# A Mamba block with a mixture of experts: the delta product in bf16, the routing's top two in PSUM, other instruction orders and banks, and 40 idle transposes at the start

## The reference

```python
xi, res = jnp.split(layernorm(x) @ W_in, 2, axis=-1)      # 256 channels each
u = silu(causal_conv4(xi) + conv_b)
dbc = u @ W_x                                             # 8 delta ranks, 16 B, 16 C
delta = softplus(dbc[..., :8] @ W_dt + b_dt)
h_t = exp(delta * A) * h_(t-1) + delta * B_t * u_t        # 16 states per channel, over t
y = (sum over states of h_t * C_t + u * D) * silu(res)
x = x + y @ W_out
s, idx = top_k(layernorm(x) @ gate_w.T, 2); p = softmax(s)
x = x + sum over the two of p * (silu(xn @ w1[e].T) @ w2[e].T)
```

## Time and profile before

| | us |
|---|---|
| median of 3 runs | 1202.45 (1202.15 to 1203.94) |
| the profiled execution | 1212.32 |
| its span, first to last instruction | 1210.5 |

### The profile page before, as it was taken

The page is one execution under the profiler, slowest core; times in us unless marked ns, Lnnn a source line. Parts: engine busy times, 40 slices in busy tenths (PEclk is TensorE's granted clock), DMA queues, the critical chain, the costliest instruction groups (busy, mean ns, idle before and its releaser), DMA issues.

```text
span 1210.5 us, 18554 instructions
## 1 busy us (share of the span) xinstructions
PE 1095.6 (91%) x6112; PEld 763.5 (63%) x6112; DVE 1045.3 (86%) x1043; ACT 889.8 (74%) x1349; POOL 966.2 (80%) x896
## 2 busy tenths in 40 slices
PE   4576879999999999999999989999999999887887
PEld 2245466675666676666768666676767666665654
DVE  2499999999999999999989999999999999998211
ACT  4887777876798797778879877889888687863232
POOL 4487887979699897879799796979988888887432
PEclk9788999999999999999999999999999999999999
DMA  4240404030030404022040402121212112020000
GB/s 140 78 158 1 158 1 158 10 140 19 27 141 10 158 10 157 0 91 74 9 157 9 157 10 108 50 88 70 87 71 87 70 51 108 1 87 1 10 9 9
DMA packets 38339, 84.10 MB, mean 69 GB/s; under 512 B 4344, under 2 KB 29184, under 8 KB 29952
## 3 DMA queue, kind: packets, MB, share of 16 engines
q1 hardware_dynamic: 36752, 83.00, 18.8%
q10 hardware_dynamic: 1520, 0.34, 0.1%
HBM read 78.62 MB, written 4.72 MB: 69 GB/s over the span
## 4 chain that ended last, share of the span: by engine, by line
PE 65%; DVE 20%; issue 11%; ACT 3%; POOL 1%; DVEq 0%; POOLq 0%; ACTq 0%
PE work L1030 18%; PE work L1020 14%; DVE h L732 12%; PE y_ps L972 10%; PE work L899 9%; DVE rows L722 3%; PE rows L951 3%; PE work L942 2%; PE work L918 2%; PE work L993 2%; PE work L909 2%; DVE yT L763 1%; PE work L883 1%; DVE weighted L806 1%; DVE top_no L797 1%
## 5 line engine op out<-in xcount | busy, mean ns | idle before, releaser
L414 POOL TENSOR_TENSOR h<-h,c_rows 128x1024 f32<-128x1024 f32 x256 | 601.2, 2367 | 44.4 <-DVE h L732 44.4
L732 DVE TENSOR_TENSOR_SCAN h<-dA,rows 128x1024 f32<-128x1024 f32 x256 | 575.8, 2271 | 0.8 <-ACT dA L620 0.7
L722 DVE TENSOR_TENSOR rows<-du,rows 128x1024 f32<-128x1024 f32 x256 | 306.6, 1215 | 37.4 <-PE rows L951 24.7
L620 ACT ACTIVATE dA<-delta,a_neg 128x510 f32<-128x510 f32 x512 | 324.7, 710 | 1.5 <-issue 0.6
L1020 PE MATMUL work<-x2T,w 128*128 128x512 f32 x512 | 265.7, 617 | 31.0 <-DVE weighted L806 15.0
L972 PEld LDWEIGHTS y_ps<-ident,h 128*128 128x128 f32 x2048 | 242.2, 145 | 49.0 <-issue 41.5
L972 PE MATMUL y_ps<-ident,h 128*128 128x128 f32 x2048 | 268.1, 280 | 0.0
L1030 PEld LDWEIGHTS work<-w,hid 128*128 128x128 f32 x2048 | 247.8, 198 | 29.3 <-ACT hid L650 15.9
L1030 PE MATMUL work<-w,hid 128*128 128x128 f32 x2048 | 254.3, 281 | 4.8 <-DVE yT L763 3.8
L650 ACT ACTIVATE hid<-work 128x512 f32<-128x512 f32 x256 | 151.4, 595 | 134.5 <-PE work L1020 133.1
L454 POOL TENSOR_TENSOR x<-x,weighted 128x512 f32<-128x512 f32 x128 | 163.2, 1275 | 75.3 <-DVE weighted L806 70.2
(11 more groups left out here) (94 smaller groups left out, 950.0 us busy)
## 6 DMA issues: line engine op xcount, KB each, us to landing
c_rows<-c_dram SPq DMA_DIRECT2D x64, 1024.0 KB, 5.0
x_in<-in_x SPq DMA_DIRECT2D x16, 256.0 KB, 2.9
x_again<-in_x SPq DMA_DIRECT2D x16, 256.0 KB, 7.3
out<-x SPq DMA_DIRECT2D x16, 256.0 KB, 2.3
w<-in_w1T SPq DMA_DIRECT2D x1, 1024.0 KB, 6.0
w<-in_w2T SPq DMA_DIRECT2D x1, 1024.0 KB, 8.1
h<-in_conv_w SPq DMA_DIRECT2D x1, 512.0 KB, 4.9
c_dram<-bcd SPq DMA_DIRECT2D x16, 32.0 KB, 5.1
```

The costliest lines, as they stand in the source:

```text
L414: nc.gpsimd.tensor_tensor(at, at, c_rows[:, n, :].unsqueeze(1).broadcast_to([P, H, T]), ALU.mult).then_inc(c_used, 1)
L620: last = nc.scalar.activation(two_seqs(dA[:, n % RING, half, :])[:, :, 1:], two_seqs(delta[:, half, :])[:, :, 1:], ACT.Exp, scale=a_neg[:, ...
L722: nc.vector.tensor_tensor(rows[:, n % 2], du[:, j.odd], rows[:, n % 2, H - 1, :].unsqueeze(1).broadcast_to([P, H, T]), ALU.mult).then_inc( ...
L732: nc.vector.tensor_tensor_scan(h[:, n % RING].rearrange("p h t -> p (h t)"), dA[:, n % RING].rearrange("p h t -> p (h t)"), rows[:, n % 2] ...
```

## The change

Five things change, some of them in all engines.

The product for delta. The 8 delta rows of `W_x` are loaded six times into `w_bc`, so that `project_bcd` puts them beside B in the free rows of the three parts, and the same splitting makes three bf16 parts of them. `w_dt` becomes two bf16 matrices of 96 rows, whose high, middle and low parts VectorE makes at the start from six loads of `W_dt`. `delta_rank` is two bf16 products on 96 rows in place of one f32 product on 8 rows, and it waits for `low`.

The selection. `top` lies in PSUM, in the bank of the scores, and `best` is copied from there; the bank is free only after `top_at_ready`. `top_numbers` is gone from VectorE; ScalarE makes `top_no` behind `ratio_exp`.

Orders and banks. All engines have new `round_(i)` lists, with less distance between the stages, and new tables of banks. The table of exp and ln is loaded where the last one was silu, and softplus shares one load.

The start. The product for `w_conv` waits for `rstd`. TensorE runs 40 transposes of the identity, which nobody reads, before it waits for the weights.

```diff
-DT_ROW = 3 * SPLIT
-C_ROW = DT_ROW + RANK
+DT_ROWS = (NS, NS + RANK)
+C_ROW = 3 * SPLIT
-CONV = (0, 1)
-GATE = (0, 1)
+CONV = (1, 0)
+GATE = (1, 1)
-DT = (1, 0)
+DT = (0, 1)
-HIDDEN = ((0, 1), (0, 1), (1, 0), (1, 1), (1, 0), (0, 1), (1, 0), (1, 0))
-EXPERT = (0, 1, 0, 1, 0, 0, 1, 0)
+HIDDEN = ((0, 1), (0, 1), (1, 0), (0, 0), (1, 0), (0, 1), (0, 0), (1, 0))
+EXPERT = (0, 1, 1, 0, 1, 1, 0, 1)
...
-        top = sb("top", [P, TB, 8])
+                top = work[:, SCORE, TB * E:2 * TB * E].rearrange("p (b e) -> p b e", b=TB)
...
+            for part in range(3):
+                for row in DT_ROWS:
+                    load(w_bc[:, :, part * SPLIT + row:part * SPLIT + row + RANK],
+                         W_x[:, 0:RANK].rearrange("(h p) n -> p h n", p=P))
...
             def delta_rank(j, half, *uses):
-                pe.wait_ge(bcd_ready, j.count(1, 1))
+                if j.loop is None and j.at == 0:
+                    pe.wait_ge(dt_weights_ready, 2)
+                pe.wait_ge(low_ready, j.count(1, 1))
                 free(*uses)
-                nc.tensor.matmul(work[:, DT[half], :], w_dt[DT_ROW:C_ROW, half * P:(half + 1) * P],
-                                 bcd[DT_ROW:C_ROW, :], start=True, stop=True).then_inc(dt_projected, 1)
+                for step in range(2):
+                    last = nc.tensor.matmul(work[:, DT[half], :], w_dt[:, step, half * P:(half + 1) * P],
+                                            parts[:, j.odd, :], start=(step == 0), stop=(step == 1))
+                last.then_inc(dt_projected, 1)
...
             def use_scores(j):
-                return (top_ready, j, 1, 1)
+                return (top_at_ready, j, 1, 1)
...
             def ratio_exp(j):
+                exp_tables()
                 act.wait_ge(top_gap, j.count(1, 1))
                 nc.scalar.activation(ratio[:, :], ratio[:, :], ACT.Exp).then_inc(ratio_ready, 1)
+                act.wait_ge(top_at_ready, j.count(1, 1))
+                nc.scalar.activation(top_no[:, :, :], top_at[:, :, 0:2], ACT.Copy).then_inc(top_no_ready, 1)
...
-                top_numbers(six)
-                scan(four, 2)
+                weight_expert(four, 0)
+                inputs(two, 6)
+                scan(two, 5)
+                weight_expert(four, 1)
...
             pre_stats(Round(0))
+            dve.wait_ge(rstd_ready[0], 1)
...
             pe.wait_ge(constants_ready, CONSTANTS)
+            for _ in range(WARM):
+                nc.tensor.transpose(y_ps[:, 0, 0, :], ident[:, :], ident[:, :])
```

More of the change, by code:

```diff
@@ L697, in round_ @@
[L697 to L708 removed]
+                one, two, three, four = (i.later(-k) for k in (1, 2, 3, 4))
+                decay(two, 14)
@@ new lines, in round_ @@
+                low(one)
+                hidden(four, 3, 0)
+                gate_silu(one, 0)
+                soft_parts(one, 0)
+                gate_silu(one, 1)
+                hidden(four, 3, 1)
+                hidden(four, 4, 0)
+                hidden(four, 4, 1)
+                soft_parts(one, 1)
+                soft_exponential(one)
+                decay(two, 15)
+                soft_log(one)
+                hidden(four, 5, 0)
+                hidden(four, 5, 1)
+                hidden(four, 6, 0)
@@ L710, in _ @@
+                decay(one, 12)
+                decay(one, 13)
+                middle(i)
             act.wait_ge(a_ready, 1)
[L711 removed]
+            run(act, round_, 4)
         @block.vector
@@ L790, in top_two @@
                 last.then_inc(top_at_ready, 1)
-            def top_numbers(j):
-                if not there(j):
-                    return
-                dve.wait_ge(top_at_ready, j.count(1, 1))
-                wait(dve, routing_step, j.count(ROUTING, 0))
-                nc.vector.tensor_copy(top_no[:, :, :], top_at[:, :, 0:2]).then_inc(top_no_ready, 1)
             def weight_expert(j, e):
@@ L854, in round_ @@
-                inputs(four, 2)
-                inputs(four, 3)
-                top_numbers(six)
-                scan(four, 2)
+                two, three, four, five = (i.later(-k) for k in (2, 3, 4, 5))
+                scan(three, 6)
+                inputs(three, 7)
+                weight_expert(five, 2)
+                inputs(three, 8)
+                scan(three, 7)
+                residual(four)
+                scan(three, 8)
+                next_pre_stats(i)
+                inputs(three, 9)
@@ new lines, in round_ @@
+                inputs(three, 15)
+                top_two(four)
+                inputs(two, 0)
+                scan(three, 15)
+                weight_expert(five, 6)
+                scan(two, 0)
+                inputs(two, 1)
+                scan(two, 1)
+                inputs(two, 2)
+                weight_expert(five, 7)
+                scan(two, 2)
+                inputs(two, 3)
+                inputs(two, 4)
+                scan(two, 3)
+                gating(three)
+                scan(two, 4)
```

439 lines of the change are left out of this document (210 added, 229 removed).

## The result

| | before | after |
|---|---|---|
| median of 4 runs | 1202.3 us | 1130.2 us (1129.7 to 1132.2) |
| ratio | 1 | 0.942 (95% 0.937 to 0.946) |
| span of the profiled execution | 1210.5 us | 1127.9 us |
| first scan starts | 48.7 | 44.2 |
| three light rounds | 180.6 | 180.5 |

The kernel is 5.8% faster: 72 us by the medians, 82.6 by the two profiled spans. I had forecast 1150 in 1129 to 1176. The time holds; of its steps several do not. The five last rows of the table split the 82.6 us: 4.5 at the start, 0.1 in the light rounds, 66.2 in the twelve full rounds, 2.0 in the last and 9.8 in the tail.

A forecast was written before the change was run, and what follows sets the result against it. TensorE was taken as the bound. Twelve rounds -36, start -7.2, light rounds and last -4, tail -8.6 gave -55.8, from 1212.3 to 1156.5 profiled; 1150 us for the median, own range 1135 to 1168, 8 in 10 1129 to 1176.

The forecast's parts named there:

- TensorE's need, 64.9 us a round: Full rounds of before: TensorE's own time from two nearly wait-free rounds, less listed waits; 63.7 after the dt change.
- rival 2: Selection fails to do what it says, or new orders wait as much elsewhere: 1175 to 1183 us; chance 0.11.
- Slow clock, 1.4 to 0.1 a round: Full rounds: eight low-clock stretches go with dt's 8-row products, three with the long copies; loss falls from 1.4 to 0.1.
- Orders and banks, 1.95 us of waits a round: Full rounds: TensorE waits for ScalarE, whose table loads stand behind waits of silus; 1.95 us, bounds 0 and 4.9.
- Rival 3: ScalarE becomes the bound, each of 10 table switches keeping it twice its row: 71.5 us a round, 1215; chance 0.03.
- Part (a): Start: the product for `w_conv` moves behind `rstd`, four more loads on ScalarE's queue; -1.0 us, between 0 and -1.5.
- Part (b): Start: 40 idle transposes keep the first convolutions from beginning slowly; 2.5 us gained.
- (c): Start: `project_bcd` goes ahead of the gates and of the next round's turn; -2.5 us.
- (d): Start: dt behind `low` +2.1, one table load fewer in softplus -1.3, scan sooner behind softplus -2.0 us.
- Light rounds and last, -4: Four rounds outside the twelve, called VectorE's, with shorter copies: a third of a full round's gain each, -4 us.
- Tail, -8.6: Behind the last scan: one expert left before the last sum, -6.4 us; new banks in both mixtures, -2.2 us.
- rival 1: Nothing waits: the loads fall into ScalarE's idle time, a round of 63.8, 1127 us; chance 0.12.

The follow-up runs named there:

- dt_eight_rows: Kernel after with dt as one f32 product of 8 rows for each half again, bf16 weights not built: 1164.7 us, ratio 0.975.
- before_new_selection: Kernel before with only the maxima in PSUM and the cast of the indices on ScalarE: 1177.5 us, ratio 0.986.
- tensor_less: Kernel after without the second half of the hidden units in the products of experts 1, 4 and 7: 1120.0 us, ratio 0.937.
- vector_more: Kernel after with four more statistics on VectorE behind each of the two groups of four, on a constant: 1147.7 us, ratio 0.960.
- old_orders: Kernel after with the lists and banks of before and no idle transposes; new selection and dt kept: 1155.9 us, ratio 0.967 to before.
- old_selection: Kernel after with maxima in SBUF and the index cast on VectorE again, behind a scan of the next round: 1181.5 us, ratio 0.987.
- six_more_loads: Kernel after with two further ScalarE table loads ahead of the decays of states 0, 7 and 11 each: 1253.3 us, ratio 1.046.
- no_idle: Kernel after without the 40 idle transposes at the start: 1130.6 us, ratio 0.944.

## Why the prediction was right, and where it was not

- **TensorE's need, 64.9 us a round: mis-sized by 0.7 to 0.9.** dt_eight_rows has the same products as before and runs whole rounds in 64.2 us, waits included; 62.8 and the 1.2 for dt give 64.0. I took two rounds of before less their listed waits; what no row lists as a wait stayed in it.
- **"TensorE is the bound", VectorE "not being the bound": wrong.** With a need of 62.8+1.2 = 64.0 TensorE stood below VectorE's 783.5/12 = 65.3 us in the kernel before, and that figure held the 2.9 us of copy and cast. The selection took VectorE to 750.8/12 = 62.6, under TensorE's 64.0 (before_new_selection), and 19 us came back by the medians where I had put only waits. In before each waited for the other: in the twelve rounds TensorE 19.7 us for scans and `weighted`, VectorE 41.0 us for TensorE. tensor_less and vector_more show that both engines bound in after; for before it is argued from these numbers, no run shows it.
- **Selection: mechanism right.** 0.17 us in all 16 rounds; rival 2 is out. By the Trainium skill ("VectorE: DVE Perf Modes", Why PSUM operands drop a tier) an operand in PSUM keeps a copy from using both SBUF read ports. The 0.17 us fit that; no run here shows the ports.
- **dt, 1.2 us a round: right.** 1.05 went to 0.43 for each half; the profiles of old_orders and before_new_selection give 1.2, dt_eight_rows against after 1.4.
- **Slow clock, 1.4 to 0.1 a round: the size right, the cause at best half.** My windows lay 2 us too early. The one at 266.80 in the earlier trace rows reads 0.80 because it holds only the start of the low stretch, which is this:

```profile
268.80:272.20 3.40, 3.40 (x17) 3.25 (x17) 1.82 (x2) 3.35 (x6) 3.40 (x3) 0.50 1.01 383
```

So the products of dt ran at the high level (their records stand 0.53 us apart), and the clock fell behind them, at the sums. Eight of the 11 stretches begin there, with no listed wait of TensorE in the 8 us before, and so do the four of before_new_selection, in four of twelve rounds. But dt_eight_rows, where the halves of dt stand 5.7 us apart, has one in twelve rounds; old_selection has 20.6 us low and six_more_loads 58.0 without any 8-row product. These products are neither enough nor needed. Waits go with a low clock more often than not (58.0 us low with 6.8 us of waits a round, 37.5 with 2.5, 20.6 with 3.1, 13.7 with 1.1, 6.8 with 1.0, none with 0.5), though not strictly: in vector_more TensorE is idle 1.0 us a round and never low. Why the stretches began at dt in the earlier trace rows stays open.

- **Orders and banks, 1.95 us of waits a round: the step that failed most.** It is 0.5, and in the even rounds next to nothing. I charged each load, as standing behind the wait of its silu, to TensorE. In two of the twelve rounds it is so, and dt waits as long as I had it (1.04 us for 0.95):

```profile
257.23 1.28 ACT L675 ACT_TABLE_LOAD   x1 [1.26 <-PE work L1058]
259.26 0.59 PE L979 MATMUL work<-parts,w_dt 96*128 96x512 bf16 x2 [1.04 <-ACT hid L675]
```

In an even round the same load runs beside the product that its silu waits for, and dt follows at 637.53 without a wait:

```profile
635.46 1.28 ACT L675 ACT_TABLE_LOAD   x1
635.49 1.13 PE L1058 MATMUL work<-x2T,w 128*128 128x512 f32 x2
```

Only eight loads in the twelve rounds wait for a product of `hidden` at all, 6.5 us, and none of them in the even rounds; why these rounds differ is open. A round is 62.75+0.5 = 63.2 instead of 65.75; of the 2.5 us, 1.45 are waits, 0.95 the need and 0.1 the clock.

- **ScalarE busy 57.7 us a round, not a bound: right in the number** (459.0/504.2x62.8 = 57.2). Rival 3's price is refuted, each load costs 1.28 (and "twice its row" would have been 57.7+12.8 = 70.5 a round, not the 71.5 that I wrote); the figure of draining in the Trainium skill ("ScalarE: Activation LUTs", What ACT_TABLE_LOAD costs) does not appear: six_more_loads has 1283 ns in each added row and 0.1 us of idle time in all before 21 of them, and in after the silu starts at 636.75, as the load from 635.46 ends. But I called idle time room, and there was none.
- **Start, -7.2: measured -4.5.** Part (a), -1.0, was +0.9: `xn` behind the longer queue. Part (b), -2.5, is 0 (no_idle). Up to `project_bcd` it is -3.0 (27.38 to 24.41) where (a) to (c) have -6.0, behind it -1.5 where (d) has -1.2. Yet one kernel's first scan lies at 44.2 or 46.4, so single executions tell this to 2 us.
- **Light rounds and last, -4: -2.1. Tail, -8.6: -9.8**, the last sum 3.6 us behind the last scan instead of 5.0.
- **The sum.** By the profiled spans -82.6 instead of -55.8, with 66.2 for 36 in the twelve rounds. The forecast of 1150 missed the median by 20 us; what came out is nearest to rival 1, "nothing waits" at 1127, and that rival was the better description.

## What to carry to other kernels

Take an engine's need from the distances between its instructions in a stretch without waits, form by form, and do so for every engine near the bound; two rounds less their listed waits gave 0.7 to 0.9 us too much and hid that VectorE needed more. Idle time of an engine is room only if work can be put there without moving what others wait for: add a known amount and measure. When low clock stretches begin at one instruction, lay the window on the slow records themselves, and take that instruction away before blaming it.

## What the runs showed of the hardware

- A VectorE copy from SBUF to SBUF beside GpSimd's products takes 0.17 to 5.41 us, the same copy out of PSUM 0.165 to 0.169 in every round of the 12 kernels that have it.
- An f32 product on 8 rows keeps TensorE 1.05 us, on 128 rows 0.86, at the same full clock, and the second of the transposes behind it comes 0.06 later still. Fewer rows are not cheaper.
- A table load is 1.283 us in every row, also in pairs, without anything behind it; a repeated load of the same set isn't emitted.
- The granted clock was low for 58.0 us of twelve rounds when TensorE waited 6.8 us a round (six_more_loads), and for none when it waited 0.5 (after).
